# Relation table of a four-layer graph network: tile-sized stores from GpSimd's queue in place of 512 KB stores from SyncE

## What is computed

```
seg = edge_dst * R + edge_type                       # R = 40 relations
S   = segment_sum(h[edge_src], seg)                  # [n, r, d]
agg = einsum('nrd,rdf->nf', S, relation_weights) + cnt @ rFeatures
h   = relu(agg*norm + (agg*norm) @ loop_weight)
```

## Time and profile before

| | us |
|---|---|
| median of three runs | 12190.51 |
| lowest and highest | 12188.19, 12197.02 |
| the profiled execution, its own time | 12153.88 |
| its span, first to last instruction | 12152.0 |
| mean granted clock of TensorE, share of full | 0.713 |

### The profile page before, as it was taken

One profiled execution on the slowest core, in us unless ns is written; L12 is line 12 of the kernel. 1 busy time (PEld: TensorE's weight loads), 2 busy tenths in 40 slices (PEclk: granted clock), 3 DMA queues, 4 the chain that ended last, 5 costly groups with the idle time before them and its releaser, 6 DMA issues. The chain is left out here.

```text
span 12152.0 us, 198157 instructions
## 1 busy us (share of the span) xinstructions
PE 6929.4 (57%) x41381; PEld 5175.5 (43%) x41382; DVE 7092.0 (58%) x19002; ACT 3369.7 (28%) x10770; POOL 5647.4 (46%) x5161
## 2 busy tenths in 40 slices
PE   4444433333366666787455553555547777777775
PEld 3211112222222222444344442444437676767675
DVE  7422235454554544777544445444448888888888
ACT  0000000000100000121111111333337776777775
POOL 0466656666255554333355553555543343434342
PEclk9767765555655555998655555666669999999998
DMA  0222234444355556554122222333345454545454
GB/s 21 79 105 107 112 95 104 103 105 102 72 156 155 154 155 144 186 180 131 45 58 58 58 58 47 95 97 95 96 86 164 143 163 142 164 143 163 143 163 122
DMA packets 1108605, 1387.92 MB, mean 114 GB/s; under 512 B 277722, under 2 KB 974382, under 8 KB 1108142
## 3 DMA queue, kind: packets, MB, share of 16 engines
q1 hardware_dynamic: 955182, 1090.46, 28.7%
q0 software_dynamic: 153344, 296.65, 11.9%
HBM read 1002.58 MB, written 383.96 MB: 114 GB/s over the span
## 5 line engine op out<-in xcount | busy, mean ns | idle before, releaser
L2097 POOL TENSOR_TENSOR msg_r<-zo_r,ex_r 128x1024 f32<-128x1024 f32 x580 | 1121.6, 1934 | 1878.2 <-ACT ex_r L2184 1878.2
L2192 ACT ACTIVATE hots_r<-zo_r,tot_r 128x128 f32<-128x128 uint8 x4640 | 1416.5, 387 | 576.0 <-DVE tot_r L2137 389.4
L2225 PE MATMUL ps<-msg_r,hots_r 128*128 128x128 f32 x9280 | 1195.2, 282 | 573.9 <-ACT hots_r L2192 461.4
L2225 PEld LDWEIGHTS ps<-msg_r,hots_r 128*128 128x128 f32 x9280 | 1087.6, 193 | 681.5 <-DVE u_sum L2150 666.5
L598 POOL DMA_INDIRECT ring_e<-t_tab,st_e x880 | 831.1, 944 | 893.5 <-DVE st_e L590 597.2
L2213 PE MATMUL ps<-u,wide_r 128*128 x9280 | 1143.2, 277 | 169.2 <-ACT wide_r L2177 164.8
L1879 POOL DMA_INDIRECT z_r<-x_tab,st_r x880 | 833.9, 948 | 808.3 <-issue 441.2
L477 POOL DMA_INDIRECT rec_tab<-st_pay,st_row x832 | 808.6, 972 | 858.3 <-DVE st_pay L529 596.7
L2213 PEld LDWEIGHTS ps<-u,wide_r 128*128 128x128 f32 x9280 | 1093.8, 194 | 171.8 <-issue 171.7
L1078 POOL DMA_INDIRECT ring_m<-t_tab,st_m x880 | 842.8, 958 | 684.9 <-issue 349.4
L598 POOL DMA_INDIRECT ring<-y_tab,st x880 | 883.4, 1004 | 550.5 <-DVE st L590 290.4
(11 more groups left out here) (316 smaller groups left out, 13040.7 us busy)
## 6 DMA issues: line engine op xcount, KB each, us to landing
zo_r<-zo_tab SPq DMA_DIRECT2D x2320, 192.0 KB, 2.6
y_tab<-y_out SPq DMA_DIRECT2D x250, 512.0 KB
k_tab<-ring_m SPq DMA_DIRECT2D x220, 520.0 KB
ring_e<-k_tab SPq DMA_DIRECT2D x220, 520.0 KB
ohts_e<-oht_tab SPq DMA_DIRECT2D x440, 128.0 KB
zo_tab<-z_r SPq DMA_DIRECT2D x220, 256.0 KB
dl_b<-dl_tab SPq DMA_DIRECT2D x220, 128.0 KB
oht_tab<-ohts SPq DMA_DIRECT2D x220, 128.0 KB
```

The source lines that it names most:

```text
L2097: nc.gpsimd.tensor_tensor(msg[:, s % WR].rearrange("p c (k d) -> p c k d", d=CD), z_of(s).rearrange("p c (k d) -> p c k d", d=CD), ex[:, s ...
L2192: last = nc.scalar.activation(hots[:, s % WR, c, :], rows[:, c, :], ACT.Copy, scale=tot[:, s, c:c + 1])
L2225: last = nc.tensor.matmul(ps[:, 4 + s % 2, c // 2 * D:(c // 2 + 1) * D], hots[:, s % WR, c, :], msg[:, s % WR, c, :], start=c % 2 == 0, st ...
```

## The change

`y_out` becomes two buffers of a whole tile (20 KB a partition each, 40 KB in place of 8). The stores leave SP. POOL now issues one store a tile (2.62 MB), right behind a batch of the scatter: batch t, wait until all ten groups of tile t are added, store of tile t, batch t+1. The last two batches follow the loop without a store between. DVE waits for a landed store once a tile, at its first group, and for the store of two tiles earlier. Matmuls, adds, staging and scatters stay as they are.

```diff
-            y_out = sb("y_out", [P, 2, 2, 512], fp32, ph)
+            y_out = sb("y_out", [P, 2, R * D], fp32, ph)
...
-                    with sp.Fori(0, NTP // 2) as i:
-                        for g in range(GRP):
-                            c = g % (GRP // 2)
-                            sp.wait_ge(s_yc, i * (2 * GRP) + (2 * g + 2))
-                            sp.dma_start(y_view[bass.ds(2 * i + g // (GRP // 2), 1), :, c * 1024:(c + 1) * 1024]
-                                         .rearrange("t p w -> (t p) w"),
-                                         y_out[:, g % 2].rearrange("p a w -> p (a w)"))\
-                              .then_inc(s_yo[g % 2], 16)
-                    for s in range(2):
-                        sp.wait_ge(s_yo[s], 16 * (NTP * GRP // 4))
...
-                    with pool.Fori(0, HB // 2) as i:
+                    def scatter(i, s):
+                        pool.wait_ge(s_st, i * 4 + (2 * s + 2))
+                        pool.sem_inc(s_tick, 1)
+                        for j in range(SU):
+                            nc.gpsimd.indirect_dma_start(
+                                out=rec_tab, out_offset=bass.IndirectOffsetOnAxis(ap=st_row[:, s, j:j + 1], axis=0),
+                                in_=st_pay[:, s, j, :], in_offset=None,
+                                bounds_check=SLOTS - 1, oob_is_err=False).then_inc(s_sc[s], 16)
+                    with pool.Fori(0, NTP // 2) as i:
                         for s in range(2):
-                            pool.wait_ge(s_st, i * 4 + (2 * s + 2))
+                            scatter(i, s)
+                            pool.wait_ge(s_yc, i * (2 * GRP) + (s + 1) * GRP)
                             pool.sem_inc(s_tick, 1)
...
+                            pool.dma_start(y_view[bass.ds(2 * i + s, 1), :, :].rearrange("t p w -> (t p) w"),
+                                           y_out[:, s, :]).then_inc(s_yo[s], 16)
+                    for i in range(NTP // 2, HB // 2):
+                        for s in range(2):
+                            scatter(i, s)
                     for s in range(2):
                         pool.wait_ge(s_sc[s], 16 * SU * (HB // 2))
+                        pool.wait_ge(s_yo[s], 16 * (NTP // 2))
...
-                        d = g // 2
-                        if g % 2 == 0 and (d >= 2 or not isinstance(i, int)):
-
-                            dve.wait_ge(s_yo[d % 2], i * (16 * GRP // 2) + 16 * (d // 2))
-                        v.tensor_tensor(y_out[:, (g // 2) % 2, g % 2, :], ps[:, g % 4, :],
-                                        rf_b[:, (g % GRP) * 512:(g % GRP + 1) * 512], ALU.add).then_inc(s_yc, 1)
+                        a, w = g // GRP, slice(g % GRP * 512, (g % GRP + 1) * 512)
+                        if g % GRP == 0 and not isinstance(i, int):
+                            dve.wait_ge(s_yo[a], i * 16)
+                        v.tensor_tensor(y_out[:, a, w], ps[:, g % 4, :], rf_b[:, w], ALU.add).then_inc(s_yc, 1)
```

## The result

The changed kernel takes 12425.24 us (median of four runs, 12391.73 to 12437.06); beside it the kernel before took 12193.76. It is 231 us slower, where 249 were forecast. The ratio on record is 1.0174, with a 95% interval of 1.016 to 1.0189; the quotient of the two medians is 1.0190. The profiled execution took 12391.73 us, 237.9 more than that of before.

The account below looks back on a forecast made before the run. POOL's queue was taken to bound 85% of the block; 50 chained rounds of 29.0 us, plus 39.6, 13.7 and 3.8, end it 248.7 us later: 12439 us, 2.0% slower. The range runs from below 12339, about 12300, to 12665.

Parts of the forecast that it names:

- The bound and the chain: Scatter block: POOL's queue bounds 85%; after the change batch, landing, staging, six adds and store run without overlap, 29.0 us a tile.
- Last scatter to the tenth add's end: Each round: landing, stagings and adds, the last two groups set by PE's four matmuls, 7.7 us.
- POOL's wake: Each round: from the end of DVE's instruction to the start of POOL's DMA, 0.86 us.
- The store: Each round, on POOL's queue: taken as a scatter's 1.28 us, with ends of 0 and 5.2 us.
- DVE's wait for the landing: Sign in the changed trace: DVE waits for the scatter's landing in every tile, some 10 us.
- The 13.7 us of late scatters: Scatter block: a scatter comes 1.96 us late seven times, 13.7 us in all.
- The end of the block: From the block's end to the next block's first DMA: 3.8 us, counted from the last scatter's start.
- Late increments in the chain: Rival: PE's increments arrive late after each batch, up to 4.5 us more a tile, 225 us, 12664 us; chance 0.14.
- A dear store: Rival: the store costs POOL 5.2 us instead of 1.28, 195 us more in all, 12634 us; chance 0.13.
- PE's upper level: Rival: the chain's four matmuls run at PE's upper clock, 2.0 us less a round, 12339 us; chance 0.06.
- By the size of the store: Rival: larger stores remove all 91.5 us of DVE's waits for stores, 12099 us; chance 0.01.
- The faster side: Rival: batch t+1 runs beside tile t's adds, POOL unstalled, 115 us sooner, 12075 us; both faster cases together 0.04.

Follow-up runs that it names:

- e11: Kernel before plus only POOL's wait for the ten adds of a tile ahead of the next batch, stores still on SP: 12356.41 us against 12146.67, ratio 1.0166.
- e8: Changed kernel with DVE's staging moved behind the tenth add, in a session with late increments: 12106.16 us against the kernel before's 12146.67, ratio 0.9956.
- e4: Kernel before plus only POOL's wait for the ten adds, in a session without late increments: 11540.49 us against 11140.59, ratio 1.0357.
- e1: Changed kernel with DVE's staging moved behind the tenth add, in a session without late increments: 11138.47 us against the kernel before's 11140.59, ratio 1.000.
- e12: Kernel before, POOL waiting behind each batch until its 16 scatters have landed, session without late increments: 11228.89 us against 11128.97, ratio 1.0092.
- e7: Kernel before with the larger y_out and one 2.62 MB store a tile, issued by SP: 12188.44 us against 12212.63, ratio 0.9981.
- e3: Kernel before with POOL paced by the landings of earlier scatters, session without late increments: 11127.91 us against 11140.59, ratio 0.9989.
- e10: Kernel before with POOL paced by the landings of earlier scatters, session with late increments: 12118.78 us against 12146.67, ratio 0.9979.
- e6: Kernel before, unaltered, run again for its trace: 12216.96 us against 12212.63, ratio 1.0006.
- e2: Changed kernel with staging behind the tenth add and POOL paced by landings, session without late increments: 11143.21 us against the kernel before's 11140.59, ratio 1.0002.
- e5: Changed kernel, unaltered, run again: 12418.91 us against the kernel before's 12212.63, ratio 1.0178.
- e9: Changed kernel with staging behind the tenth add and POOL paced by landings, session with late increments: 12086.48 us against the kernel before's 12146.67, ratio 0.9945.

## Why the prediction held

**The bound and the chain.** POOL bounded the block and the new wait made a chain without overlap: shown, by the wait alone (e11, 1.0166) and by cutting the chain in one place (e8, 0.9956, with the same stores in the same queue).

**The terms of the round,** as means of the 50. The batch, 15 steps: 19.2 us for 19.1. Last scatter to the tenth add's end: 7.8 for 7.7. POOL's wake: 0.76 for 0.86. The store: 0.58 with a gap of 0.30 or, in some rounds, 0.64 behind it, on average 1.04 us for 1.28; it is shorter than a scatter, and the case of five pieces a row is out. Sum 28.7 for 29.0, 13 us less over 50 rounds. DVE's waits for the small stores, whose end the prediction took to give nothing in the chain, may be worth up to 0.20 us of it, by e4 and e11. Of the signs, DVE's wait for the landing was mis-sized: 860.1 / 48 = 17.9 us a tile, not some 10, since DVE has its first four adds done early in the batch.

**The 13.7 us of late scatters** were a wrong term. The seven scatters that come 1.96 us late do not occur in the changed kernel, nor in e1 and e8, which have the same 50 stores among their scatters. e4, e11 and e12, without stores on POOL, have all seven, at the same places in the row; e7 has four of them and two that are 1.4 us late; e3, where POOL never waits for staging, has none. In the kernel before each of the seven is the second scatter behind a wait of POOL of some 6.7 us. Why is open.

**The end of the block** was 3.6 us too short: the next block begins 7.4 us behind the last scatter's start. In the earlier trace rows the 3.8 us lie behind the last add, and I put them behind the wrong event. Together: 248.7 - 13 - 13.7 + 3.6 = 225.6, what the block measured.

**Behind the block** I had nothing. Up to the block of the last section the changed kernel needs 5.7 us more than the kernel before, in that block 17.0 less, and behind it 23.8 more; together they are the 12.3 us within 0.2. The two outer stretches, with the blocks in which POOL gathers, vary from trace to trace by 50 and 40 us in the sessions with late increments, so no cause can be read from them.

**Luck.** Two errors made the forecast too high (13 and 13.7 us) and two too low (3.6 and 12.3), so that the 237.9 us of the profiled execution lie only 10.8 from the 248.7. The chain was right by its mechanism; that the sum is as close as this is in part chance.

**The rivals.** Late increments in the chain: not one in this block of the changed kernel, and none in e11. Both have a rest of 7 to 8 us for POOL in each round; that the rest is what keeps them away fits, but was not tested by itself. A dear store: no. PE's upper level: no, PE's four matmuls take 3.78 us at 931.93 as in tile 0, and so in 42 of the 50 rounds, 3.4 to 3.6 in the others. The granted clock of PE from 500 to 900 us was 0.67, below the 0.70 of the earlier trace rows:

```profile
500.00:900.00 400.00, 168.62 (x294) 66.30 (x294) 95.46 (x166) 8.21 (x28) 225.01 (x238) 0.67 0.24 93
```

By the size of the store: no, e7 has the larger stores without the wait and is 0.2% faster, not 0.75%.

The faster side needed the batch to run beside the adds. The order of the changed kernel forbids it; e1 and e8 show what it would have given, 21.1 us a round in one kind of session and 23.8 in the other. My 12075 for it left out that an unbroken POOL brings the late increments back: e8 is 12106 beside a before of 12147, 40 us less, not 115.

**What the prediction didn't know** is that the kernel before has two speeds by session. In the other one the wait alone costs twice as much (e4). Its account, that late increments cost the kernel before little since POOL covers them, was too mild as well: against the 20.4 us a round of the other sessions (e3) it has 3.8 us more, 188 us in this block.

## What to carry to other kernels

Before a transfer is moved to another engine's queue, write down what that engine's next instruction is and what the transfer waits for. If the transfer waits for work that itself waits for that engine, the two run in turn, whatever their durations; here one wait cost 1.7 to 3.6%, and moving the staging six adds later gave it back. The size of a store that nobody waits for for long (e7) was worth 0.2% here, and its size and queue together (e8) 0.4%.

## What the runs showed of the hardware

**Late increments while POOL scatters.** Where they occur, DVE or ACT waits for a semaphore increment of a matmul that ended long before, while POOL issues indirect DMAs one behind another. In the kernel before:

```profile
939.48 3.69 PE L507 MATMUL ps<-w,xt 128*128 128x512 f32 x8 [2.01 <-ACT xt L493]
...
959.34 0.69 DVE L523 TENSOR_TENSOR y_out<-ps,rf_b 128x512 f32<-128x512 f32 x1 [4.13 <-remote]
...
973.15 0.42 PE L501 MATMUL ps<-ident,xs 128*128 128x128 f32 x1
...
992.31 0.28 ACT L493 ACTIVATE xt<-ps 128x128 f32<-128x128 f32 x1 [52.59 <-remote]
```

The eight matmul records are a tile's first four groups and end at 943.17; the add at 959.34 is that of the fourth, 16 us later. ACT's copy begins 18.7 us behind the end of the transpose that it reads; the 52.59 us in brackets are ACT's idle time, most of it from before that matmul. Over the block the adds with such a wait start 4 to 21 us behind their group's last matmul (median 13), while DVE's idle time before each is 4.2 us in the median and at most 6.2. They need no stores from SP (e8), and they don't hang on how far POOL's sequencer has run ahead, between 13 and 6 (e10). They are absent from this block where POOL rests 7 to 8 us a round (the change, e11); further on in the same trace of the change, where POOL gathers, DVE still waits 418 us for them. Whether a rest of 1.5 us would do is open, and so is the mechanism.

**They come with the session, not with the kernel.** e1 and e8 are one kernel: 11138 us without them, 12106 us with them. In this block the difference is 1651.7 - 1513.3 = 138 us; nearly all of the rest lies in three of the four later blocks in which POOL gathers (239, 259 and 328 us from first to last gather, 12 in the fourth). What sets it no run tells. The chip's number does not: the record has number 15 for e8 to e11, with late increments, and for e12, without them.

**A plain DMA of 128 rows of 20 KB occupies POOL for 0.58 us,** an indirect one of 128 rows of 16 bytes for 0.97. The store's row is in the result above, the scatter's in the earlier trace rows.

**A block far behind the change got shorter.** In it POOL, DVE and PE form messages from the second layer's heads; its matmuls run, in the kernel before,

```profile
L1394 PE MATMUL ps<-msg_e,hots_e x1760: 382/383/794, 4892.9 to 5703.2; 128*128 128x260 f32 x196
```

for 810.3 us, and in the changed one,

```profile
L1390 PE MATMUL ps<-msg_e,hots_e x1760: 382/383/772, 5124.0 to 5917.5; 128*128 128x260 f32 x196
```

for 793.5 us, 17 us less, with unchanged code. The whole block takes 849 to 852 us in the five traces of the kernel before, e4, e6, e11 and e12, 841 and 843 in e3 and e10, and 832 to 835 in the seven with the larger `y_out` (the change, e1, e2, e5, e7, e8, e9). In both groups it is steady to 3 us, in both kinds of session. The cause was not sought.
